# A hybrid transformer layer: stores and sums ahead of the head loads, wider memsets beside two norms, queries projected first

## The reference

```python
x = x + time_mix(_layernorm(x))
x = x + ffn(_layernorm(x))        # F
x = x + latent_attention(_layernorm(x))   # L, causal, 16 heads of 8
x = x + ffn(_layernorm(x))        # H

def ffn(x):
    h = layernorm(x, ln1_g, ln1_b)
    q, k, v = h @ Wq, h @ Wk, h @ Wv          # 16 heads of 8
    attn = softmax(q @ k.T / sqrt(8))         # over 2048 keys, not causal
    x = x + (attn @ v) @ Wo
    m = layernorm(x, ln2_g, ln2_b)
    # 8 experts of 512, the two best of each token weighted and summed
    return x + moe(m)
```

## Time and profile before

| | us |
|---|---|
| three executions, median | 3222.56 |
| the profiled execution | 3221.15 |
| its span | 3219.4 |
| PE busy | 2728.3 (85%) |
| DVE busy | 2021.2 (63%) |
| ACT busy | 1852.0 (58%) |
| POOL busy | 407.5 (13%) |
| mean granted TensorE clock | 0.896 of full speed |

### The profile page before, as it was taken

One profiled execution on the slowest core, in us unless ns is written; L12 is line 12 of the kernel. 1 busy time (PEld: TensorE's weight loads), 2 busy tenths in 40 slices (PEclk: granted clock), 3 DMA queues, 4 the chain that ended last, 5 costly groups with the idle time before them and its releaser, 6 DMA issues. The chain is left out here.

```text
span 3219.4 us, 63170 instructions
## 1 busy us (share of the span) xinstructions
PE 2728.3 (85%) x21001; PEld 1132.2 (35%) x21001; DVE 2021.2 (63%) x4035; ACT 1852.0 (58%) x2211; POOL 407.5 (13%) x664
## 2 busy tenths in 40 slices
PE   6788838988888889799699999949888889887998
PEld 2688832222222222344334433422222222222443
DVE  5544467877777777321488777648777778774222
ACT  4222205877777778434246656637777778776343
POOL 1222231111111111000011211101111111110000
PEclk9888857999989989899889999978989989898999
DMA  1000003111111011121111111121011011110211
GB/s 42 1 0 0 0 1 113 34 32 43 31 35 43 26 39 39 46 64 52 58 47 57 48 49 57 45 87 60 29 40 39 26 43 35 30 43 24 77 59 33
DMA packets 93530, 130.80 MB, mean 41 GB/s; under 512 B 17969, under 2 KB 60939, under 8 KB 90827
## 3 DMA queue, kind: packets, MB, share of 16 engines
q1 hardware_dynamic: 87509, 119.87, 12.0%
q10 hardware_dynamic: 5744, 7.17, 0.7%
HBM read 90.28 MB, written 23.89 MB: 35 GB/s over the span
## 5 line engine op out<-in xcount | busy, mean ns | idle before, releaser
L685 ACT ACTIVATE Fprob<-Fs 128x1024 f32<-128x1024 f32 x512 | 518.0, 1028 | 158.1 <-PE Fs L537 131.3
L685 ACT ACTIVATE Hprob<-Hs 128x1024 f32<-128x1024 f32 x512 | 518.0, 1028 | 154.2 <-PE Hs L537 126.6
L762 DVE TENSOR_REDUCE Fmaxes<-Fm 128x1 f32<-128x512 f32 x744 | 471.9, 683 | 70.2 <-PE Fm L597 61.1
L762 DVE TENSOR_REDUCE Hmaxes<-Hm 128x1 f32<-128x512 f32 x744 | 472.0, 683 | 67.6 <-PE Hm L597 58.2
L762 DVE TENSOR_REDUCE Lmaxes<-Lm 128x1 f32<-128x512 f32 (+3 forms) x640 | 354.5, 603 | 92.3 <-PE Lm L521 57.7
L685 ACT ACTIVATE Lprob<-Ls 128x1024 f32<-128x1024 f32 (+7 forms) x384 | 293.4, 778 | 168.8 <-PE Ls L537 106.3
L569 PE MATMUL Fo<-Fprob,Fvh 128*32 128x256 f32 x4096 | 338.4, 410 | 0.3 <-ACT Fprob L685 0.3
L569 PE MATMUL Ho<-Hprob,Hvh 128*32 128x256 f32 x4096 | 335.1, 406 | 0.3 <-ACT Hprob L685 0.3
L597 PE MATMUL Fm<-ka,Fqa 60*128 60x512 bf16 x744 | 235.6, 402 | 96.5 <-DVE Fmaxes L762 88.2
L597 PE MATMUL Hm<-ka,Hqa 60*128 60x512 bf16 x744 | 235.4, 402 | 95.3 <-DVE Hmaxes L762 87.5
L537 PE MATMUL Fs<-Fqa,ka 60*128 60x512 bf16 x1024 | 270.0, 404 | 1.6 <-ACT Fprob L685 1.6
(11 more groups left out here) (445 smaller groups left out, 3875.5 us busy)
## 6 DMA issues: line engine op xcount, KB each, us to landing
FEwb<-FE_weights SPq DMA_DIRECT2D x8, 1024.0 KB, 5.7
HEwb<-HE_weights SPq DMA_DIRECT2D x8, 1024.0 KB
Fvh<-vstack SPq DMA_DIRECT2D x17, 256.0 KB, 2.5
Lvh<-vstack SPq DMA_DIRECT2D x17, 256.0 KB, 2.4
Hvh<-vstack SPq DMA_DIRECT2D x17, 256.0 KB, 2.4
FEw<-in_L_ffn_W SPq DMA_DIRECT2D x16, 256.0 KB, 2.9
HEw<-in_L_ffn_W SPq DMA_DIRECT2D x16, 256.0 KB
Fqa<-F_qparts SPq DMA_DIRECT2D x34, 96.0 KB
```

The lines of the kernel that those rows point to most:

```text
L685: nc.scalar.activation(prob[:, :, :].rearrange("p k q -> p (k q)")[:, lo:hi], sps[entry_slot(h, "score", a, n)][:, o:o + hi - lo], ACT.Exp ...
L762: nc.vector.reduce_max(maxes[:, a, t, kb:kb + 1], src[:, 0:n], AX.X).then_inc(max_free, 1)
```

## The change

There are three edits. Memsets: `ka` and `pairs` are now set over all 128 partitions by one instruction each, in F's N1, and `vstack`, `topp` and `nothing` are set in F's N2. Projection of F and H: the order of the blocks is queries, pairs, keys; SP stores the queries and loads head 0's queries, then its pairs; ACT stores the pairs and the keys. Heads of F and H: SP does `spread(h - 1)` ahead of the wait for the weighing and of `load(h + 2)`, as it did already in L. L's own order is unchanged; the three semaphores `stored` are only made at another place.

```diff
-    BLOCKS = [(2, b) for b in range(NB)] + [(w, b) for w in (0, 1) for b in range(NB)] if PAIRED \
-        else [(w, b) for w in (1, 0) for b in range(NB)]
+    BLOCKS = [(w, b) for w in ((0, 2, 1) if PAIRED else (1, 0)) for b in range(NB)]
...
                     for half in range(2):
-                        if n == ends(0, half):
-                            store(act, 0, half)
-                if not PAIRED:
+                        if PAIRED and n == ends(2, half):
+                            store(act, 2, half)
+                        if PAIRED and n == ends(1, half) or not PAIRED and n == ends(0, half):
+                            store(act, 1 if PAIRED else 0, half)
+                if PAIRED:
+                    store(act, 1, 1)
+                else:
                     store(act, 0, 1)
...
                 if PAIRED:
-                    store(sp, 2, 0)
-                    store(sp, 2, 1)
+                    store(sp, 0, 0)
+                    store(sp, 0, 1)
+                    sp.wait_ge(stored[0], 32)
+                    load_q(sp, 0, 0)
                     sp.wait_ge(stored[2], 32)
                     load_pairs(sp, 0, 0)
-                    sp.wait_ge(stored[0], 32)
-                    load_q(sp, 0, 0)
-                    store(sp, 1, 0)
-                    store(sp, 1, 1)
                     sp.wait_ge(stored[1], 32)
...
                 def head(h, u, first=False, last=False):
-                    if causal and not first:
+                    if not first:
                         spread(h - 1)
                     if not last:
 
                         if not first:
                             sp.wait_ge(weighed, RING + NK * h)
                         load(h + 2, (u + 2) % SLOTS)
-                    if not first and not causal:
-                        spread(h - 1)
                     if not first:
                         keep(h - 1)
...
-        fill = [(consts[n][:][64 * r:64 * r + 32], v) for n, v in (("ka", -1.0), ("pairs", 0.0)) for r in range(GROUPS)]
-        fill += [(consts[n][:], v) for n, v in (("vstack", 1.0), ("topp", 0.0), ("nothing", 0.0))]
+        fill = [[(consts[n][:], v) for n, v in values]
+                for values in ((("ka", -1.0), ("pairs", 0.0)), (("vstack", 1.0), ("topp", 0.0), ("nothing", 0.0)))]
 
-        def feed_forward(name, fill=None):
+        def feed_forward(name, fill=(None, None)):
 
-            normalize(nc, name + "N1", x, n1, None, consts, fill=fill)
-            normalize(nc, name + "N2", n1, n2, main, consts, col["ln1_g"], col["ln1_b"])
+            normalize(nc, name + "N1", x, n1, None, consts, fill=fill[0])
+            normalize(nc, name + "N2", n1, n2, main, consts, col["ln1_g"], col["ln1_b"], fill=fill[1])
```

More of the change, by code:

```diff
@@ L118, in attention @@
     K_LOADS = 16 * GROUPS * PARTS
+    stored = [semaphore(nc, heads, f"{name}{x}_stored") for x in ("q", "k", "pairs")]
     FIRST_ROW = [TROWS + sum(PARTS - b for b in range(a)) * DH for a in range(PARTS)]
@@ L166, in attention @@
             sem(x) for x in ("projected", "split", "high", "middle", "second", "mixed", "padded", "v_read"))
-        stored = [sem(f"{x}_stored") for x in ("q", "k", "pairs")]
         def store(engine, w, half):
```

## The result

The changed kernel takes 3022.19 us (median of four executions, 3019.81 to 3024.42), against 3222.28 us before. The ratio is 0.938, with a 95% interval of 0.936 to 0.939. The forecast was 2987 us, with a range from 2962 to 3045: 235 us less were forecast, and 200 were measured.

The account below looks back on a forecast made before the run. VectorE's mid-head wait for the sums was taken to stop the whole pipeline and halve the clock. Heads 212, memsets 10.4 and projection 13 save 235 us of 3221.15, giving 2986, predicted as median 2987 us; range 2962 to 3045.

Parts of the forecast that it names:

- The stall goes: Heads of F and H: sums land at 881.2, VectorE asks at 890.85, 9.7 us to spare, so its wait disappears.
- The loads become late: Rival, heads of F and H: delayed loads land after TensorE asks, say 3250 us; chance 0.02.
- The pace of a head: Heads of F and H without the stop: 40.3 us each, range 39.4 to 41.5.
- three banks cover only part of it: Division in each head: VectorE's 1.3 us is partly covered by three banks, costing the chain between 0 and 1.3 us.
- the subtraction in the prediction: Head of F: 48.87 us between exponentials less stalls of 7.27, 0.96 and 0.56 gives 40.1, division not included.
- The count from the window of 560 to 600: F, stretch without a stop: 392 matmuls in 40.00 us, 386 per head, so 39.4 us a head.
- The jumps: Loop jumps in three of thirteen periods of F and H: 3.5 us added per jump, range 2.3 to 6.
- The first stall and the slow clock behind the last one: Outside the thirteen-period windows of F and H: 5.5 us saved per attention, bounds 1.5 to 7.9.
- The memsets: F's N1 and N2: N1 13.4 us shorter, N2 3.0 us later, net gain 10.4 us, bounds 6 to 13.4.
- The projection: Projection to head 0, F and H: head 0 starts 6.5 us earlier (4 to 8) in each, 13 in both.
- The start without GpSimd's sum: Projection's first matmul: queries need no sum of halves, so splits start 2 us earlier (1 to 2.6).
- The clock: Rival, heads of F and H: ring waits keep the clock at 0.9, a head takes 42.6, total 3051 us; chance 0.10.

Follow-up runs that it names:

- p_dose: Changed kernel with stores and fetch of sums put behind 17 of the 21 loads of a later head, in F and H: 3114.3 us, ratio 0.9655.
- p_norecip: Changed kernel with the reciprocal left out of every division, so the output is not the attention's: 2979.12 us, ratio 0.9235.
- p_unroll: Changed kernel with TensorE's loop over heads 3 to 14 written out in all three attentions: 3014.17 us, ratio 0.9355.
- p_unroll2: Changed kernel with the loops over heads 3 to 14 written out on TensorE and VectorE: 2971.34 us, ratio 0.920.
- p_proj: Kernel before with only the new order of projection, stores and first loads: 3220.05 us, ratio 0.9973.

## Why the prediction was right, and where its sizes were off

**The stall goes: right.** The sums land ahead of VectorE's question in every head but the last, 9.2 us ahead in the head shown, where 9.7 was forecast. p_dose shows both sides of it: the wait is the arrival less the question, 1.9 us where the rows of before gave 1.8, since 11.5 us of loads put ahead of the stores overdraw the spare time.

**The loads become late: no.** TensorE waits for no load in the middle of the attentions; the new delay of 5.3 us was covered, as worked out.

**The pace of a head: the term that was mis-sized.** The forecast took 40.3 us out of bounds from 39.4 to 41.5; 41.2 was measured. The step that failed is "three banks cover only part of it" with "I take 40.3": nothing of the reciprocal is covered. By p_norecip the rest of a head, the product included, is 40.1 us, just what the subtraction in the prediction gave. So the reciprocal of 0.94 us costs 1.1 us. The count from the window of 560 to 600, 39.4, was too low, since it holds only part of a head. Over 26 periods the 0.9 us make 23 us of the missing 35.

**The jumps: mis-sized too.** I took 3.5 us per jump from TensorE's wait and an allowance for the clock behind it; the long periods of F and H have 3.5 to 5.3 us over the others. p_unroll and p_unroll2 show that two engines stand at their own jumps at nearly the same time, and that the clock falls behind that. Six jumps make 5 us more than forecast. The first stall and the slow clock behind the last one were worth 3.4 to 4.0 us per attention, not 5.5.

**The memsets: right.** 11.1 us against 10.4. N1 takes 12.1 us, and in N2 one `tensor_scalar` is locked for 2.91 us where I had 3.0; VectorE's sixteen in N1 end at 457.9, 3.7 us behind GpSimd's end at 454.2, where I had 4.2. (By the rule of the Trainium skill, page "SBUF — State Buffer", section "Who interferes with whom", of GpSimd and a VectorE instruction in a two-port mode the one that issues second waits for the other's whole instruction. The trace agrees, with a `tensor_scalar` of 16 columns that takes 2.91 us beside `vstack` and ends within 0.1 us of it; the same one takes 0.18 us in the kernel before.)

**The projection: the direction right, the size 8.2 against 13.** What head 0 waits for last is the pairs, as forecast, in F with 6.8 us on TensorE. But it starts 27.2 us after the first matmul in F and 25.2 in H, and not 24. Three estimates were too good. The start without GpSimd's sum was to give 2 us and gave 1.3, since 1.29 us of the wait of 2.59 are left. The queries were to be split by 495, counted with even blocks, but the fourth block of the kernel before is split only at 498.6; on the same time scale it now comes at 496.7 in H and at 498.2 in F, where TensorE's first matmuls ran at the low clock. And SyncE's eight loads of queries took 7.2 us in F (485.84 to 493.08) where they had taken 4.8, with ScalarE's stores of pairs and keys, 768 KB each, in flight beside them. They take 7.0 to 7.2 us in H and in p_proj too; that it is the stores which slow the loads is argued from their place in time and was not tried by itself.

**The clock: the rival that did not come.** With the stall gone the granted clock is 0.98, and 1.00 once the jumps are gone too, although TensorE keeps its short waits on the ring of banks, the longest of them 0.9 us in p_unroll2. What is left of the slow clock within the thirteen periods of the changed kernel lies behind the three jumps: a period with a jump has 0.93 to 0.96.

**The whole.** Of the 34 us by which the two profiled executions' spans missed the forecast, the pace makes 23, the jumps 5, the first stall and the clock behind the last one 4, and the projection 5; the memsets (1) and the other stages (2) went the other way. The four terms all erred to the same side, and the range held the result because it had kept 41.5 us per head as a bound.

## What to carry to other kernels

A wait that an engine off the critical path makes in the middle of its row is priced by what stands behind it: here 4.5 us of VectorE cost 6.5 to 6.8 us per head (the windows of thirteen periods, before and after), as TensorE runs one fixed order and comes back at half its clock. On a queue that is in order, put the few transfers that somebody waits for ahead of the many that are for later, and count how long the later ones can wait. And try a long instruction on an engine that feeds a ring in pieces that the ring covers, even when that makes its work larger: 0.94 us was not covered here, four times 0.34 us was.

## What the runs showed of the hardware that I had not expected

Waits of TensorE of 2.3 to 3.9 us at the divisions of p_dose were each followed by half the clock, so that a wait of VectorE costs nearly twice its length (3.2 us per period for 1.8 us). A memset on GpSimd costs the same over 32 rows as over 128: 10.48 us for two of `ka`'s quarters before, 5.22 for the whole after. At a jump of a loop TensorE stands 2.0 to 2.6 us in F and H and 2.9 to 3.9 in L, and VectorE 2.2 to 3.1 us once TensorE's loop is written out. The profile shows no releaser for it but issue, and what the engine waits for stays open. Writing out the loops of two engines took 50 to 58 us off the kernel, more than the memsets and the projection together.
